# Raw attention scores as sixteen 32x32 products a step, with a wait of TensorE on its own signal ahead of the mask products

## The reference

```python
allowed = (adj > 0) | (jnp.swapaxes(adj, 1, 2) > 0) | eye
q, k, v = jnp.split(x @ Wqkv.T + bqkv, 3, axis=-1)      # 8 heads of 16
scores = jnp.einsum('bhqd,bhkd->bhqk', q * scale, k)
scores = jnp.where(allowed[:, None], scores, -jnp.inf)
attn = jax.nn.softmax(scores, axis=-1)
ctx = jnp.einsum('bhqk,bhkd->bhqd', attn, v)
x = _layernorm(x + ctx @ Wo.T + bo, ln1_g, ln1_b)
x = _layernorm(x + jax.nn.relu(x @ W1.T + b1) @ W2.T + b2, ln2_g, ln2_b)
```

## Time and profile before

| | |
|---|---|
| runs | 1477.68, 1479.81, 1483.33 us; median 1479.81 |
| span of the profiled execution, first to last instruction | 1257.3 us (the profile states no time of its own beside it) |
| median above that span | 222.5 us |
| TensorE busy | 1051.1 us, 84% of the span |
| TensorE weight loads busy | 407.3 us, 32% |
| ScalarE busy | 805.9 us, 64% |
| VectorE busy | 809.0 us, 64% |
| GpSimd busy | 737.5 us, 59% |
| mean granted clock of TensorE | 0.933 of 2.4 GHz |

### The profile page before, as it was taken

The page is one execution under the profiler, slowest core; times in us unless marked ns, Lnnn a source line. Parts: engine busy times, 40 slices in busy tenths (PEclk is TensorE's granted clock), DMA queues, the critical chain, the costliest instruction groups (busy, mean ns, idle before and its releaser), DMA issues.

```text
span 1257.3 us, 29309 instructions
## 1 busy us (share of the span) xinstructions
PE 1051.1 (84%) x10998; PEld 407.3 (32%) x10998; DVE 809.0 (64%) x3062; ACT 805.9 (64%) x1031; POOL 737.5 (59%) x741
## 2 busy tenths in 40 slices
PE   0136687688993989999999999999999999999874
PEld 0122331243331433343434333434343334333222
DVE  7866887758778476977797869776364534122323
ACT  1221257677852767788878887888768756875541
POOL 4776677567777777777777777777777520000000
PEclk9556789899997899999999999999999999999996
DMA  6523336416322534353435343532242210000000
GB/s 188 167 69 105 93 103 158 147 53 137 119 83 80 140 85 135 104 121 85 131 112 115 87 129 107 120 86 62 78 69 71 55 52 18 18 3 10 10 9 8
DMA packets 95157, 110.77 MB, mean 88 GB/s; under 512 B 17081, under 2 KB 75969, under 8 KB 94977
## 3 DMA queue, kind: packets, MB, share of 16 engines
q1 hardware_dynamic: 68352, 62.67, 16.4%
q0 software_dynamic: 22816, 44.61, 15.6%
q10 hardware_dynamic: 3808, 1.19, 0.4%
HBM read 91.10 MB, written 12.85 MB: 83 GB/s over the span
## 4 chain that ended last, share of the span: by engine, by line
PE 63%; ACT 11%; DVE 9%; POOL 7%; issue 6%; DMA 3%; DVEq 0%; POOLq 0%; ACTq 0%; SPq 0%
PE sc L1673 20%; PE cb L1693 13%; ACT probs L1469 10%; PE sc L1677 7%; PE m L1749 5%; PE m L1757 4%; POOL nb_low L716 3%; POOL nb_low L694 3%; PE m L1579 2%; PE m L1602 2%; PE sc L1715 1%; DMA nb_low<-h_rows,lsorted 1%; PE m L1731 1%; PE m L1607 1%; PE m L1779 1%
## 5 line engine op out<-in xcount | busy, mean ns | idle before, releaser
L1469 ACT ACTIVATE probs<-sc 128x1024 f32<-128x1024 f32 x512 | 496.5, 1022 | 247.6 <-PE sc L1677 245.6
L694 POOL DMA_INDIRECT nb_low<-h_rows,lsorted x474 | 470.1, 992 | 172.3 <-issue 126.1
L1693 PE MATMUL cb<-probs,va 128*17 128x512 f32 x2048 | 272.3, 604 | 4.8 <-issue 4.1
L1673 PE MATMUL sc<-q_near,k_g 32*128 32x512 f32 x1024 | 147.8, 644 | 21.7 <-ACT probs L1469 18.5
L1673 PE MATMUL sc<-q_far,k_g 32*128 32x512 f32 x1024 | 149.6, 654 | 16.3 <-ACT probs L1469 15.9
L1016 DVE TENSOR_REDUCE agg<-nb_low 128x128 f32<-128x1024 f32 (+10 forms) x58 | 96.4, 1662 | 54.3 <-DMA nb_low<-h_rows,lsorted 31.5
L1677 PE MATMUL sc<-barred,negident 32*32 32x512 bf16 x4096 | 112.9, 388 | 0.3 <-issue 0.2
L830 DVE MAX8 cand<-keys 128x8 f16<-128x128 f16 x512 | 105.4, 279 | 2.2
L716 POOL DMA_INDIRECT nb_low<-h_rows,first_lists x80 | 80.1, 1001 | 42.5 <-issue 23.2
L1677 PEld LDWEIGHTS sc<-barred,negident 32*32 32x32 bf16 x4096 | 35.4, 88 | 198.6 <-issue 198.6
L1461 ACT ACTIVATE barred<-m 128x512 bf16<-128x512 f32 x128 | 73.4, 610 | 40.6 <-PE m L1607 40.6
(11 more groups left out here) (182 smaller groups left out, 1457.6 us busy)
## 6 DMA issues: line engine op xcount, KB each, us to landing
adj_t<-in_adj_dram SPq DMA_DIRECT2D x64, 512.0 KB
nb_low<-h_rows,lsorted POOLq DMA_INDIRECT x474
xh<-in_x_dram SPq DMA_DIRECT2D x8, 512.0 KB
h_rows<-xh SPq DMA_DIRECT2D x8, 512.0 KB
hl<-h_rows SPq DMA_DIRECT2D x8, 512.0 KB
x<-in_x_dram SPq DMA_DIRECT2D x16, 256.0 KB
out_dram<-h2T SPq DMA_DIRECT2D x16, 256.0 KB
ag<-pooled_rows SPq DMA_DIRECT2D x7, 512.0 KB
```

The source lines that it names most:

```text
L694: pool.indirect_dma_start(out=dst, out_offset=None, in_=h_rows[0:(f + 1) * (N + 1), :], in_offset=bass.IndirectOffsetOnAxis(ap=lsorted[:, ...
L1469: nc.scalar.activation(probs[:, i % 2, 2 * pair:2 * pair + 2, :], sc[:, 2 * pair:2 * pair + 2, :], ACT.Exp, scale=SCALE).then_inc(s_probs, 1)
L1673: nc.tensor.matmul(sc[:, a, :], k[part, :], q[part, :], start=True, stop=False)
L1693: last = nc.tensor.matmul(cb[a * SPAN:a * SPAN + VW, :], va[:, u % 2, a, kt, :], probs[:, i % 2, a, :], start=(kt == 0), stop=(kt == T - 1))
```

## The change

The loop over heads at line 1673 gets an inner loop over four groups `c` of 32 key columns: the product of head `a` and columns `c` runs in the 32x32 tile at row group `a` and column group `c`, and writes 32 partitions of bank `a`. The last of the sixteen raises a new semaphore, and TensorE waits for it ahead of the first mask product.

```diff
+        s_raw_scores = sem("raw_scores")
@@ def scores(g, n)
                     for a in range(GROUP):
                         part = slice(a * SPAN, (a + 1) * SPAN)
-                        nc.tensor.matmul(sc[:, a, :], k[part, :], q[part, :], start=True, stop=False)
+                        for c in range(GROUP):
+                            cols = slice(c * SPAN, (c + 1) * SPAN)
+                            last = nc.tensor.matmul(sc[cols, a, :], k[part, cols], q[part, :], start=True, stop=False)
+                    last.then_inc(s_raw_scores, 1)
+                    pe.wait_ge(s_raw_scores, i + 1)
```

## The result

| | before | changed |
|---|---|---|
| median | 1479.4 us | 1652.9 us |
| ratio | | 1.117, interval 1.115 to 1.120 |
| span of the profiled execution | 1257.3 us | 1656.5 us |
| TensorE products, records | 10998 | 17142 |

Slower, as forecast, but by 173 us where 34 were forecast, and outside the range (1471 to 1580). The two spans of the table must not be subtracted: the kernel before takes about 1258 us in some sets of runs and 1471 to 1480 in others (the quick and the slow level from here on), and the profile that the prediction read was of the first, the runs of the result of the second. Kernels are compared within one set of runs only. All runs of a set had the same level; it is not a matter of the chip, for two chips showed both.

What follows compares the result with a forecast made beforehand. The loop from raw products through masks to exps was taken as the bound; +0.14 us a step for 240 steps gives +34 us, span 1291, plus the 222.5 us carried over, so 1514 us, range 1471 to 1580.

Steps and rivals of the forecast that it cites:

- What bounds the kernel: Attention steps: raw products to masks lies on every step's chain; lean step 3.54 us, about 232 steps pay, 240 taken.
- the sum: Raw products to masks: -0.08 + 0.08 + 0.14 = +0.14 us a step, +34 us for 240 steps.
- Parts one and two: Raw products: narrower loads gain 0.08 us a step, sixteen products instead of four lose 0.08; they cancel.
- the rival of dear products: Raw products: passes start 0.025 us apart, 1569 us; or later tiles start late, 1619; or no side-by-side running, above 2000; together 16%.
- short look-ahead: Raw products: TensorE cannot look past fifteen waiting second passes, later tiles start 0.44 us late, +139 us, 1619; within a joint 16%.
- Part three: Wait between raw products and masks: 0.59 to the modelled end + 0.07 hop - 0.52 = 0.14 us lost a step.
- the signs: What a step's close-up would show: masks 1.21 us after raw products start, 0.05 to 0.08 us new TensorE idle between.
- The carried-over remainder: Whole run: 222.5 us of the median above the profiled span lies outside first and last instruction and stays unchanged.
- Gain: Raw to masks: own signal seen as quickly as the shape change, distance 0.99 us, 19 us gained, 1461; chance 12%.
- no change: Raw to masks: half of hop and spread paid, within 0.03 us a step, 1473 to 1487; chance 9%.
- the forecast alone: Attention steps: +0.06 to +0.22 us a step over 232 to 256 steps, 1495 to 1534; chance 60%.
- The clock: TensorE clock should stay at 1.00; rival: a tenth of steps at 1.2 GHz, +58 us on top, 1572; chance 3%.

Runs made afterwards that it cites:

- the wait alone: Kernel before, its four raw products kept, TensorE waiting for its own signal of them ahead of the masks: 1295.1 us quick (1.028), 1509.5 slow (1.021).

## Why the prediction was wrong

- **What bounds the kernel.** Right. Raw products, masks and exps stand in one loop, and what was added to raw to mask came back in the step: 3.82 against 3.54 in the lean one. All steps paid, where the sum had 240: 255 of them at the mean 0.31 us at the quick level.
- **Parts one and two.** Right. The raw products cover 1.15 us where they covered 1.14, and their last pass starts 0.57 us after the first, as the 0.55 of the sum; narrower loads and twelve more products cancel. At the quick level all but 4 of 206 steps took the 32 passes without holding any up, so the rival of dear products was wrong there. At the slow level some 30 steps held them up, for about 30 us in all; the gaps fall in different places of the burst, so this is not the short look-ahead of that rival.
- **Part three.** This is the term that failed at the quick level. The sum had 0.14 us: 0.59 from the second pass to the modelled end, and a hop of 0.07, less 0.52. The hop was read from a signal behind eight mask products and taken over to one behind 32 passes. With four raw products the whole cost is 0.16, so the method was sound. With sixteen it is 0.78 from the last second pass to the masks instead of 0.66, and TensorE's idle time there is 0.20 us where the signs named 0.05 to 0.08. The term should have been 0.26, with 0.01 to 0.02 more in the passes 0.28 a step, and with 255 steps that is +71 instead of +34, of the 79 measured.
- **The carried-over remainder.** This is the step that failed for the result. "That remainder lies outside the first and last instruction and is carried over unchanged": it was time inside the span, of an execution of the slow level. A gap of 222 us, 15% of the time, was a sign that the profile and the runs were of different conditions, in which the price of a signal need not be the same. It is not: with gathers at the slow level raw to mask is a further 1.17 us longer in the changed kernel (2.65 against 1.48), 1.01 of it the signal and 0.16 the raw products, and TensorE's own later work waits with it; with the four products of the wait alone it is 0.39 (1.66 against 1.27), and from masks to exps it is 0.49 shorter than before (1.02 against 1.51). The step is 0.46 us dearer than at the quick level (0.77 against 0.31), and 206 x 0.46 is the other 95 us of the 173.
- **The rivals.** Gain and no change stayed out. (By its own terms the forecast alone is 1494 to 1536, where 1495 to 1534 stands; nothing hangs on it.) The clock had a part at the slow level only, and a small one: the granted clock was 0.89 from 198 to 1420 us and 1.00 in the last graph, against 0.93 and 1.00 of the kernel before at that level. Two of the result's runs had 0.87 in the mean and two 0.90, and they took 1655 to 1658 and 1650 to 1651 us. The forecast of 1.00 held at the quick level, at 0.99 from 462 to 1130 us. No rival had a signal that is late by what stands ahead of it.

## What to carry to other kernels

When an engine must wait for its own products, price the signal by the number of instructions that stand in the burst ahead of it, not by the hop behind another burst, and ask whether a change of tile shape, which needed no wait, was the cheaper barrier, as it was here (0.52 us from the last second pass to the masks, against 0.78). Ask too what stands behind the wait in the engine's own order: a late signal to another engine leaves the sender its work, a late signal to itself does not. If the time of the runs and the span of the profile differ by more than a few us, find out first in which condition each was taken: durations of one are no prices for the other. A kernel in a tight loop of signals between two engines should be measured at both levels before one version of it is called the better.

## What the runs showed of the hardware

- Sixteen fp32 products in 32x32 tiles, two passes each, run side by side as fast as four of 32 rows by 128 columns: 1.15 us against 1.14.
- A product that waited for TensorE's own signal started 0.68, 0.71 and 0.78 us after the start of the last pass ahead of it, with 8, 16 and 32 passes in the group.
- At the slow level TensorE's signals were late by about 1 us in the mean while GpSimd executed gather instructions of 0.85 to 0.95 us, and not at all once the gathers had ended. A third of the bytes in the same number of instructions and packets left it as it was.
- Short bursts started on time in nearly all of these steps (masks 1.07 us after the raw products in the slow kernel before, as in the quick one). Long ones did not always: 25 to 33 of 206 bursts of 32 raw passes, and the bursts of 40 mask and small products for 1.21 us from first to last start instead of 0.56.
